# Cross attention of a gated block: the second exponential written over the scores in PSUM, in two halves, each split and waited for by itself

## The chip, the cores and the metric

The kernel runs on one core of a Trainium2 chip. A core has TensorE (PE in the profile; its weight loads are listed apart as PEld), VectorE (DVE), ScalarE (ACT), GpSimd (POOL) and SyncE (SP), which here only starts transfers. Matrix products land in PSUM, whose 8 banks each hold 128 x 512 numbers of 32 bits; all else lies in SBUF. The metric is the device time of one launch, in microseconds (us). The median of 3 runs before the change is 2361.93 us (2361.77 to 2367.37).

## The reference, cut to what matters

The whole is a gated cross attention, a gated feed forward part, slots with 16 experts, and a second attention, over x of 8 blocks of 512 rows by 512. The change touches the first of these:

```
xn  = layer_norm(x);  ctx = layer_norm(context)
q   = (xn @ Wq) as 16 heads of 64, * 64 ** -0.5
k,v = split(ctx @ Wkv)                      # one head of keys and values for all 16
sim = q @ k.T, -inf where mask == 0
out = softmax(sim) @ v                      # per head
x1  = x + tanh(g_xattn) * (out @ Wout)      # then the feed forward part is added
```

## The kernel before, in words

**Numbers in two parts.** TensorE reads its operands in a shortened format (fp32r). To keep the precision, each operand is kept as a high part (the rounded value) and a low part (the value minus the high part), and each product is made of two or three products of parts. For the probabilities this means: ScalarE makes the exponential once into `prob_hi` (rounded as it is written) and once more, unrounded, into `prob`; VectorE subtracts one from the other into `prob_lo`.

**Blocks and pairs.** `cross_attention` goes over 8 blocks `b`, and in each over 8 pairs of heads `i` (64 pairs in all). Of each block the mask lets at most 128 keys through (another branch, not taken here, serves other masks), so the scores of one pair are two tiles of 128 keys x 512 queries: the tile `SC` (`att_scores`), two PSUM banks, one for each head of the pair (`odd` 0 and 1). A pair takes these steps, by line of the kernel before:

- PE `pair_scores` (L642, L645): eight products into both banks of SC.
- ACT `exponentials`: L786 `prob_hi`, then L787 `prob`, each over both banks at once (128 x 1024).
- DVE `low_probs_of`: L1006 `prob_lo = prob - prob_hi`, 128 x 1024.
- PE `pair_out`: L655, L656 (twice each, from `prob_hi`), then L659 twice (from `prob_lo`) into `OB` (`att_out`). The value operand holds columns of ones, so OB holds the sums of the exponentials too.
- ACT `logarithms`, `inverses`: L794 twice, L798, which make one over the sums as exp(-ln(sum)) in `inv`.
- DVE `normalise` (L1013, twice) into `acc`; POOL L911 and L913 split `acc` into `oT_hi` and `oT_lo`, operands of the output products (L675).

**Order of the work.** Each engine has its own queue, written out by hand, and runs it strictly in order; semaphores join them. Between `pair_scores` and `pair_out` of a pair PE does the 12 query products of the next block (L591) and its maxima (L621); in the last block it does output products there (L675). ACT's order in a pair is L794, L794, L798 (of the pair before), L786, L787, then L772 (high part of the next block's queries). DVE's is L1013 twice (of the pair before), L1006, L998 (maxima), L992 (low part of the queries). After pair 7 of a block PE does the last maxima (L621) of the next block, which wait until L998 has read those before them, then turns x (L554) and makes outputs (L675).

**Semaphores that the change touches.** `probs` counts finished L787s, `low_probs` finished L1006s. PE waits for `low_probs` ahead of the first L659, and for `probs` ahead of the next `pair_scores` and of the first output products, since these overwrite SC. `prob` also serves, at the start of the program, as the place for one quarter of the raw Wq.

Of the kernel before, what the change touches and what calls it, by code (L numbers as in the profile page):

```python
# [7 lines left out]
ALU = mybir.AluOpType  # L8
ACT = mybir.ActivationFunctionType
AX = mybir.AxisListType  # L10

P = 128
B, S, D = 8, 512, 512
# [3 lines left out]
HP = H // 2  # L17
# [9 lines left out]
def plain(ap):  # L27

    return ap.bitcast(F32)


def products(hi_lo_w, hi_lo_m):

    (w_hi, w_lo), (m_hi, m_lo) = hi_lo_w, hi_lo_m
    return ((w_hi, m_hi), (w_hi, m_lo), (w_lo, m_hi))
# [280 lines left out]
def cross_attention(nc, whole, taken, I, ident, gates, many, first, x1_d, xnT_d, t_d, PIECES):  # L316
# [4 lines left out]
    with ExitStack() as stage:  # L321
        mem = Memory(nc, stage, whole, taken)
# [41 lines left out]
        m_heads = mem.sbuf("m_heads", [P, S], F32R)  # L364
        m_rows = mem.sbuf("m_rows", [P, TT, MC])
        mem.sbuf("m_rows_to_next_line", [P, LINE // 2 // 4])
        prob = mem.sbuf("prob", [P, 2, S])
        prob_hi = mem.sbuf("prob_hi", [P, 2, S], F32R)
        prob_lo = mem.sbuf("prob_lo", [P, 2, S], F32R)
        inv = mem.sbuf("inv", [P, 2, S])  # L370
        acc = mem.sbuf("acc", [P, 2, S])
        oT_hi = mem.sbuf("oT_hi", [P, HP, S], F32R)
        oT_lo = mem.sbuf("oT_lo", [P, HP, S], F32R)
        x_rows = mem.sbuf("x_rows", [P, TT, D])
        piece_place = [mem.sbuf(f"piece_{n}", [P, 4, P], F32R) for n in ("sum", "high")]

        SC, MX, OB = (pair_bank(n) for n in ("att_scores", "att_maxima", "att_out"))
        G = [mem.bank(f"att_general{i}") for i in range(2)]

        two = lambda ap: ap.rearrange("p i s -> p (i s)")  # L380
        raw_wkv = inv[:, 0, :].rearrange("p (k n) -> p k n", k=KT)
        raw_wq = [two(x_rows[:, 0:2, :]), two(x_rows[:, 2:4, :]), two(prob[:, :, :]), two(acc[:, :, :])]
        raw_wo = raw_wq[0:2]
        wkv_parts = [(slice(0, DH), slice(0, DH)), (slice(DH, 3 * DH), slice(0, P))]
        gam_rows = inv[0:2 * KT, 1, 384:384 + P]
# [28 lines left out]
        scores, hi_probs, probs, low_probs, heads_out, inv_ready, heads_taken, o_done, out_ready, x_added = (  # L414
            mem.sem(n) for n in ("scores", "hi_probs", "probs", "low_probs", "heads_out", "inv_ready", "heads_taken", "o_done", "out_ready", "x_added"))
# [25 lines left out]
        def out_banks(b):  # L441
            return [G[0][:, :], G[1][:, :], MX[:, 0, :], MX[:, 1, :]] if b >= late else [SC[:, 0, :], SC[:, 1, :], MX[:, 0, :], MX[:, 1, :]]
# [5 lines left out]
        with nc.Block() as block:  # L448
# [86 lines left out]
            def _(pe):  # L535
# [96 lines left out]
                def pair_scores(b, i):  # L632
                    pe.wait_ge(g_free, turned("q", b, i))
                    if i == 0:
                        pe.wait_ge(m_heads_ready, b + 1)
                        if 1 <= b <= late:
                            pe.wait_ge(x_added, (b - 1) * TT + 2)
                    if b or i:
                        pe.wait_ge(probs, b * HP + i)
                    for n, (kk, q) in enumerate(products((k_hi[b % 2], k_lo[b % 2]), (q_hi, q_lo))):  # L640
                        for half, odd in zip(halves, range(2)):
                            nc.tensor.matmul(SC[:, odd, :], kk[half, :], q[half, i, :], start=n == 0, stop=False)  # L642
                    for half, odd in zip(halves, range(2)):
                        at = odd * DH + i
                        last = nc.tensor.matmul(SC[:, odd, :], minus[half, at:at + 1].to_broadcast([DH, P]), m_heads[half, :], start=False, stop=True)  # L645
                    last.then_inc(scores, 1)

                def pair_out(b, i):
                    hi, lo = v_hi[b % 2], v_lo[b % 2]
                    cols = [slice(DH, 3 * DH), slice(0, P)]  # L650
                    pe.wait_ge(hi_probs, b * HP + i + 1)
                    if b or i:
                        pe.wait_ge(heads_taken, b * HP + i)
                    for odd in range(2):
                        nc.tensor.matmul(OB[:, odd, :], hi[:, cols[odd]], prob_hi[:, odd, :], start=True, stop=False)  # L655
                        nc.tensor.matmul(OB[:, odd, :], lo[:, cols[odd]], prob_hi[:, odd, :], start=False, stop=False)  # L656
                    pe.wait_ge(low_probs, b * HP + i + 1)
                    for odd in range(2):
                        last = nc.tensor.matmul(OB[:, odd, :], hi[:, cols[odd]], prob_lo[:, odd, :], start=False, stop=True)  # L659
                    last.then_inc(heads_out, 1)  # L660

                def output(b, i, tiles=range(TT)):
                    pe.wait_ge(o_done, b * HP + i + 1)
                    banks = out_banks(b)
                    for t in tiles:
                        if i == 0 and b > late:
                            pe.wait_ge(x_added, late * TT + t + 1)
                        if i == 0 and t == 0 and b == late:
                            pe.wait_ge(g_free, len(order))
                        if i == 0 and t == 0 and b < late:  # L670
                            pe.wait_ge(probs, (b + 1) * HP)
                        if i == 0 and t == 2 and b <= late:
                            pe.wait_ge(max_taken, (b + 2) * HP)
                        for n, (o, w) in enumerate(products((oT_hi, oT_lo), (wo_hi, wo_lo))):
                            last = nc.tensor.matmul(banks[t], o[:, i, t * P:(t + 1) * P], w[:, i, :],  # L675
                                                    start=i == 0 and n == 0, stop=i == HP - 1 and n == 2)
                        if i == HP - 1:
                            last.then_inc(out_ready, 1)

                def last_outputs(b):  # L680
                    pe.wait_ge(o_done, (b + 1) * HP)
                    for t in range(TT):
                        output(b, HP - 2, [t])
                        output(b, HP - 1, [t])
# [74 lines left out]
            def _(act):  # L759
# [21 lines left out]
                def exponentials(b, i):  # L781
                    bias = first_bias[:, b:b + 1]
                    act.wait_ge(scores, b * HP + i + 1)
                    if b or i:
                        act.wait_ge(heads_out, b * HP + i)
                    nc.scalar.activation(two(prob_hi[:, :, :]), two(SC[:, :, :]), ACT.Exp, bias=bias).then_inc(hi_probs, 1)  # L786
                    nc.scalar.activation(two(prob[:, :, :]), two(SC[:, :, :]), ACT.Exp, bias=bias).then_inc(probs, 1)  # L787

                def logarithms(b, i):
                    act.wait_ge(heads_out, b * HP + i + 1)  # L790
# [134 lines left out]
            def _(dve):  # L925
# [76 lines left out]
                    nc.vector.tensor_copy(m_heads[0:MC, :], OB[0:MC, 0, :]).then_inc(m_heads_ready, 1)  # L1002

                def low_probs_of(b, i):
                    dve.wait_ge(probs, b * HP + i + 1)
                    nc.vector.tensor_tensor(two(prob_lo[:, :, :]), two(prob[:, :, :]), two(plain(prob_hi[:, :, :])), ALU.subtract).then_inc(low_probs, 1)  # L1006

                def normalise(b, i):
                    dve.wait_ge(inv_ready, b * HP + i + 1)
# [2076 lines left out]
def gated_block(nc, I, out):  # L3086
# [6 lines left out]
    with ExitStack() as whole:  # L3093
# [18 lines left out]

        taken = []
        x1_begun = cross_attention(nc, whole, taken, I, ident, gates, many, first, x1_d, xnT_d, t_d, made_pieces)
        with nc.sbuf_tensor("bo_place", [P, D], F32R) as bo_place:
            pass
# [45 lines left out]
```

## Time and profile before

| | us |
|---|---|
| median of 3 runs | 2361.93 |
| the profiled execution's own time | 2363.39 |
| its span, from first to last instruction | 2361.6 |
| PE busy / share of the span | 2097.8 / 89% |
| DVE busy | 1328.9 / 56% |
| ACT busy | 673.9 / 29% |
| POOL busy | 618.8 / 26% |
| L659, the products with `prob_lo`, first and last start | 61.3, 624.8 |

The profile follows one execution. A busy share says how long an engine held work, not whether others waited for it. Matmuls overlap in their pipeline: a 128 x 512 product is shown as some 0.39 us, while the next one starts 0.23 us later, so PE can look nearly full in a stretch in which it also waits. What PE loses is therefore best read from the distance between starts.

### The profile page before, as it was taken

The numbers are of one execution on the slowest core, as the hardware profiler recorded it, in microseconds if no ns is written. First come the engines' busy times: TensorE is split into PE (matmuls) and PEld (weight loads), VectorE is DVE, ScalarE is ACT, GpSimd is POOL, SyncE is SP. The second block draws the span as 40 slices with busy tenths as digits, with TensorE's granted clock in tenths as the row PEclk, the third lists the DMA queues.
The fourth block names the chain that finished last, engine by engine and source line by source line (L and its number), as shares of the span: only waits on it lengthen the run. The fifth ranks groups of instructions, "written<-read, shape, count | busy, mean of one in ns | idle before, by whom it ended". The sixth has DMA issues, their size and how long they took to land. (4 is left out here: it accounts for less than half of the span.)

```text
span 2361.6 us, 29531 instructions
## 1 busy us (share of the span) xinstructions
PE 2097.8 (89%) x11170; PEld 1586.7 (67%) x11170; DVE 1328.9 (56%) x2127; ACT 673.9 (29%) x1068; POOL 618.8 (26%) x553
## 2 busy tenths in 40 slices
PE   7999999999989999999999999998998445454898
PEld 6777777777778788888888888887873111111577
DVE  7766666656457777667767676666651000000387
ACT  3644465446443331112111211123421000000231
POOL 5544565435377831310132000000320000000010
PEclk9999999999999999999999999999998767687899
DMA  4133223332296668665866494434879999999767
GB/s 166 70 104 131 103 65 107 118 107 74 91 393 243 240 267 338 226 207 194 340 225 212 178 357 161 160 125 167 321 289 431 433 426 432 432 433 430 277 235 264
DMA packets 181338, 565.10 MB, mean 239 GB/s; under 512 B 14256, under 2 KB 97752, under 8 KB 151352
## 3 DMA queue, kind: packets, MB, share of 16 engines
q1 hardware_dynamic: 172936, 504.37, 56.4%
q10 hardware_dynamic: 8272, 58.99, 5.9%
q8 instruction: 82, 1.34, 0.2%
q14 instruction: 48, 0.39, 0.1%
HBM read 450.07 MB, written 113.25 MB: 239 GB/s over the span
## 5 line engine op out<-in xcount | busy, mean ns | idle before, releaser
L1475 PE MATMUL ff_down<-w,u 128*128 128x512 f32 x1536 | 362.0, 394 | 8.5 <-DVE ff_x L1748 8.5
L1415 PE MATMUL ff_up<-ff_t,w 128*128 128x512 f32 x1488 | 357.6, 389 | 2.0 <-ACT ff_gate L1548 2.0
L1475 PEld LDWEIGHTS ff_down<-w,u 128*128 128x128 f32 x1536 | 291.0, 190 | 73.4 <-DVE ff_x L1748 12.6
L1415 PEld LDWEIGHTS ff_up<-ff_t,w 128*128 128x128 f32 x1488 | 279.2, 188 | 60.3 <-issue 2.4
L1748 DVE SCALAR_TENSOR_TENSOR ff_x<-ff_down,gates,ff_x 128x512 f32<-128x512 f32 x256 | 191.0, 749 | 86.8 <-PE ff_down L1475 85.3
L1415 PE MATMUL ff_up<-ff_b,w 128*128 128x512 f32 x954 | 234.3, 389 | 0.0
L2532 PE MATMUL e_down<-e_w,e_ug 128*32 128x512 f32 x480 | 74.7, 779 | 179.5 <-DMA e_w<-in_L_ffn_e_W 94.6
L1415 PEld LDWEIGHTS ff_up<-ff_b,w 128*128 128x128 f32 x954 | 179.1, 188 | 37.2
L2532 PEld LDWEIGHTS e_down<-e_w,e_ug 128*32 128x32 f32 x480 | 18.5, 138 | 234.2 <-issue 134.8
L1540 ACT ACTIVATE ff_gate<-ff_gate 128x512 f32<-128x512 f32 x62 | 39.2, 633 | 410.8 <-DVE ff_gate L1724 410.8
L2197 POOL TENSOR_TENSOR yn_lo<-y,yn_hi 128x2048 fp32r<-128x2048 f32 x8 | 36.7, 4592 | 437.6 <-ACT yn_hi L2155 437.6
L2640 DVE TENSOR_TENSOR e_u_rows<-e_turned,e_b1T 128x128 f32<-128x128 f32 x16 | 4.7, 292 | 260.0 <-PE e_turned L2523 260.0
L2985 POOL TENSOR_TENSOR v_pairs<-v_biased,c_odd_rows 128x512 f32<-128x512 f32 x2 | 2.5, 1286 | 491.7 <-DVE v_biased L3062 491.7
L1013 DVE TENSOR_TENSOR acc<-att_out,inv 64x512 f32<-64x512 f32 x128 | 88.1, 688 | 67.3 <-ACT inv L798 65.6
L913 POOL TENSOR_TENSOR oT_lo<-acc,oT_hi 128x512 fp32r<-128x512 f32 x64 | 115.2, 1801 | 9.4 <-issue 0.5
L1559 ACT COPY ff_gate<-ff_up 128x512 f32<-128x512 f32 x62 | 36.5, 589 | 271.1 <-PE ff_up L1415 271.1
L94 POOL TENSOR_TENSOR ff_t_sum<-ff_t_sum,ff_t_high 128x512 f32<-128x512 f32 x20 | 28.4, 1421 | 310.8 <-DMA ff_t_high<-xnT 310.8
L1006 DVE TENSOR_TENSOR prob_lo<-prob,prob_hi 128x1024 fp32r<-128x1024 f32 x64 | 80.2, 1253 | 52.1 <-ACT prob L787 51.9
L591 PE MATMUL att_general<-nT_hi,wq_hi 128*128 128x512 f32 x252 | 106.5, 423 | 0.4 <-DVE nT_lo L962 0.4
L794 ACT ACTIVATE inv<-att_out 64x512 f32<-64x512 f32 x128 | 75.9, 593 | 90.6 <-PE att_out L659 89.9
L2593 ACT COPY e_y_parts<-e_down 128x512 f32<-128x512 f32 x16 | 9.4, 586 | 321.1 <-PE e_down L2532 311.5
L591 PE MATMUL att_general<-nT_hi,wq_lo 128*128 128x512 f32 x252 | 99.8, 396 | 0.0
(482 smaller groups left out, 4385.9 us busy)
## 6 DMA issues: line engine op xcount, KB each, us to landing
w<-ff_w_factors SPq DMA_DIRECT2D x48, 1792.0 KB, 7.4
e_wg<-in_L_ffn_e_Wg SPq DMA_DIRECT2D x15, 4096.0 KB, 25.7
e_w<-in_L_ffn_e_W SPq DMA_DIRECT2D x14, 4096.0 KB, 20.0
e_w<-in_L_ffn_e_W ACTq DMA_DIRECT2D x13, 4096.0 KB, 50.3
ff_w_factors<-w SPq DMA_DIRECT2D x15, 1792.0 KB, 6.9
w<-ff_w_parts SPq DMA_DIRECT2D x48, 512.0 KB, 4.8
ff_t<-ff_t_factors SPq DMA_DIRECT2D x16, 1024.0 KB, 13.9
e_w<-in_L_ffn_e_W SPq DMA_DIRECT2D x16, 1024.0 KB, 9.8
```

Source lines behind the costliest of these rows:

```text
L591: last = nc.tensor.matmul(bank[:, :], w[:, k, i * P:(i + 1) * P], m[:, k, :], start=k == 0 and n == 0, stop=k == KT - 1 and n == 2)
L794: nc.scalar.activation(inv[halves[odd], i % 2, :], OB[halves[1 - odd], odd, :], ACT.Ln)
L913: nc.gpsimd.tensor_tensor(oT_lo[:, i, :], acc[:, i % 2, :], plain(oT_hi[:, i, :]), ALU.subtract).then_inc(o_done, 1)
L1006: nc.vector.tensor_tensor(two(prob_lo[:, :, :]), two(prob[:, :, :]), two(plain(prob_hi[:, :, :])), ALU.subtract).then_inc(low_probs, 1)
L1013: last = nc.vector.tensor_tensor(acc[half, i % 2, :], OB[half, odd, :], inv[half, i % 2, :], ALU.mult)
L1415: last = nc.tensor.matmul(bank[:, :], a, m, start=start and c == 0, stop=stop and c == 5)
L1475: last = nc.tensor.matmul(DN[m % 2][:, :], a, w, start=c == 0, stop=c == 5)
L1540: nc.scalar.activation(g, DN[n][:, :] if n < PLAIN else g, ACT.Silu).then_inc(gate1_done, 1)
L1559: nc.scalar.copy(gate0[n % 2][:, :], up_bank(n, A11_B11)[:, :]).then_inc(p1_kept, 1)
L1748: v.scalar_tensor_tensor(place, DN[m % 2][:, :], gates[:, 0:1], place, ALU.mult, ALU.add).then_inc(down_taken, 1)
L2197: nc.gpsimd.tensor_tensor(yn[1][:, b % 2], y[:, :, :], plain(yn[0][:, b % 2]), ALU.subtract).then_inc(yn_lo_done, 1)
L2532: last = nc.tensor.matmul(YB[q * QW:(q + 1) * QW, :], ug[:, j * Q + q, :], w2[i][:, q * J + j, :], start=j == 0, stop=j == J - 1)
```

## The change

The second exponential no longer goes to `prob` in SBUF: it is written over the scores it reads, in PSUM, as two instructions of 128 x 512, one for each head. A drain of ACT stands ahead of them, since they overwrite what the first exponential reads. DVE's subtraction is cut in two in the same way and reads SC. Each half has its own count of `probs` and of `low_probs`, so both counts run to 2 x 64, and PE waits for each half ahead of the L659 that uses it. What overwrites SC now waits for `low_probs`. The tile `prob` stays as `wq_place` with its other use alone, so that nothing else moves in memory.

```diff
-        prob = mem.sbuf("prob", [P, 2, S])
+        wq_place = mem.sbuf("wq_place", [P, 2, S])
@@ pair_scores
                     if b or i:
-                        pe.wait_ge(probs, b * HP + i)
+                        pe.wait_ge(low_probs, 2 * (b * HP + i))
@@ pair_out
-                    pe.wait_ge(low_probs, b * HP + i + 1)
                     for odd in range(2):
+                        pe.wait_ge(low_probs, 2 * (b * HP + i) + odd + 1)
                         last = nc.tensor.matmul(OB[:, odd, :], hi[:, cols[odd]], prob_lo[:, odd, :], start=False, stop=True)
@@ output
                         if i == 0 and t == 0 and b < late:
-                            pe.wait_ge(probs, (b + 1) * HP)
+                            pe.wait_ge(low_probs, 2 * (b + 1) * HP)
@@ exponentials
                     nc.scalar.activation(two(prob_hi[:, :, :]), two(SC[:, :, :]), ACT.Exp, bias=bias).then_inc(hi_probs, 1)
-                    nc.scalar.activation(two(prob[:, :, :]), two(SC[:, :, :]), ACT.Exp, bias=bias).then_inc(probs, 1)
+                    act.drain()
+                    for odd in range(2):
+                        nc.scalar.activation(SC[:, odd, :], SC[:, odd, :], ACT.Exp, bias=bias).then_inc(probs, 1)
@@ low_probs_of
-                    dve.wait_ge(probs, b * HP + i + 1)
-                    nc.vector.tensor_tensor(two(prob_lo[:, :, :]), two(prob[:, :, :]), two(plain(prob_hi[:, :, :])), ALU.subtract).then_inc(low_probs, 1)
+                    for odd in range(2):
+                        dve.wait_ge(probs, 2 * (b * HP + i) + odd + 1)
+                        nc.vector.tensor_tensor(prob_lo[:, odd, :], SC[:, odd, :], plain(prob_hi[:, odd, :]), ALU.subtract).then_inc(low_probs, 1)
```

ACT's queue over one pair of block 0, before (L794 and L798 are the logarithms and the inverse, L772 is the high part of the queries):

```order
L786 ACTIVATE prob_hi<-att_scores,first_bias 128x1024 [waits heads_out,scores]
L787 ACTIVATE prob<-att_scores,first_bias 128x1024
L772 ACTIVATE q_hi<-att_general 128x512 [waits g_ready]
L794 ACTIVATE inv<-att_out 64x512 [waits heads_taken,heads_out]
L794 ACTIVATE inv<-att_out 64x512
L798 ACTIVATE inv<-inv 128x512
```

and after the change, the same place (lines further down are numbered 2 higher):

```order
L786 ACTIVATE prob_hi<-att_scores,first_bias 128x1024 [waits heads_out,scores]
L789 ACTIVATE att_scores<-att_scores,first_bias 128x512 x2
L772 ACTIVATE q_hi<-att_general 128x512 [waits g_ready]
L796 ACTIVATE inv<-att_out 64x512 [waits heads_taken,heads_out]
L796 ACTIVATE inv<-att_out 64x512
L800 ACTIVATE inv<-inv 128x512
```

One instruction over two banks has become two over one bank each, with SC as their output; nothing has moved past anything else. The drain is not a row of the order.

PE's queue at the end of a pair and the start of the next, as the difference of the two:

```order
 L655 MATMUL att_out<-prob_hi,v_hi 128x512
 L656 MATMUL att_out<-prob_hi,v_lo 128x512
-L659 MATMUL att_out<-prob_lo,v_hi 128x512 [waits low_probs]
-L659 MATMUL att_out<-prob_lo,v_hi 128x512
-L642 MATMUL att_scores<-q_hi,k_hi 128x512 [waits probs,g_free]
+L659 MATMUL att_out<-prob_lo,v_hi 128x512 [waits low_probs] x2
+L642 MATMUL att_scores<-q_hi,k_hi 128x512 [waits low_probs,g_free]
```

The products are the same in the same order; the second L659 has a wait of its own, and the next pair's scores wait for another semaphore.

## Rows read from the trace of the kernel before

**Rows 1.** Busy time by engine, 55 to 640 us: PE, PEld, DVE, ACT, POOL, clock, DMA share, GB/s.

```profile
55.00:640.00 585.00, 574.95 (x2883) 437.32 (x2881) 369.41 (x556) 303.53 (x423) 282.08 (x242) 1.00 0.28 95
```

**Rows 2.** Who waited for whom, 55 to 630 us: total us, times, longest.

```profile
PEld att_out L659 <- DVE prob_lo L1006: 17.3, 54, 1.0
...
PE att_maxima L621 <- DVE m_rows L998: 4.3, 7, 0.6
```

**Rows 3.** Timeline of ACT and DVE, one pair of block 2: start, us, instruction, idle before.

```profile
246.45 1.20 ACT L794 ACTIVATE inv<-att_out 64x512 f32<-64x512 f32 x2 [1.30 <-PE att_out L659]
247.72 0.63 ACT L798 ACTIVATE inv<-inv 128x512 f32<-128x512 f32 x1
248.26 1.10 ACT L786 ACTIVATE prob_hi<-att_scores,first_bias 128x1024 fp32r<-128x1024 f32 x1
249.26 1.10 ACT L787 ACTIVATE prob<-att_scores,first_bias 128x1024 f32<-128x1024 f32 x1
...
252.44 0.60 ACT L794 ACTIVATE inv<-att_out 64x512 f32<-64x512 f32 x1 [1.32 <-PE att_out L659]
...
250.39 1.23 DVE L1006 TENSOR_TENSOR prob_lo<-prob,prob_hi 128x1024 fp32r<-128x1024 f32 x1 [0.62 <-ACT prob L787]
```

**Rows 4.** Timeline of PE, end of five pairs: 2.0, 1.1, 6.6, 4.3, 7.3.

```profile
221.36 0.39 PE L656 MATMUL att_out<-prob_hi,v_lo 128*128 128x512 f32 x1
...
222.13 0.50 PE L642 MATMUL att_scores<-q_hi,k_hi 64*128 64x512 f32 x2
...
150.99 0.40 PE L656 MATMUL att_out<-prob_hi,v_lo 128*128 128x512 f32 x1
...
151.81 0.50 PE L642 MATMUL att_scores<-q_hi,k_hi 64*128 64x512 f32 x2
...
562.75 0.40 PE L656 MATMUL att_out<-prob_hi,v_lo 128*128 128x512 f32 x1
...
563.59 0.50 PE L642 MATMUL att_scores<-q_hi,k_hi 64*128 64x512 f32 x2
...
391.87 0.40 PE L656 MATMUL att_out<-prob_hi,v_lo 128*128 128x512 f32 x1
...
393.15 0.50 PE L642 MATMUL att_scores<-q_hi,k_hi 64*128 64x512 f32 x2
...
597.69 0.39 PE L656 MATMUL att_out<-prob_hi,v_lo 128*128 128x512 f32 x1
...
599.01 0.51 PE L642 MATMUL att_scores<-q_hi,k_hi 64*128 64x512 f32 x2
```

**Rows 5.** One line each: how often, ns min/median/max, first and last start.

```profile
L764 ACT ACTIVATE nT_hi<-att_general,gam x28: 677/689/692, 50.9 to 502.2; 128x512 fp32r<-128x512 f32 x28
...
L772 ACT ACTIVATE q_hi<-att_general x63: 580/598/603, 23.1 to 567.8; 128x512 fp32r<-128x512 f32 x63
...
L967 DVE TENSOR_TENSOR cT_lo<-att_general,cT_hi x7: 684/692/692, 60.8 to 506.0; 128x512 fp32r<-128x512 f32 x7
...
L1006 DVE TENSOR_TENSOR prob_lo<-prob,prob_hi x64: 1224/1226/1672, 59.6 to 621.0; 128x1024 fp32r<-128x1024 f32 x64
...
L913 POOL TENSOR_TENSOR oT_lo<-acc,oT_hi x64: 1270/2083/2172, 70.9 to 629.9; 128x512 fp32r<-128x512 f32 x64
```

**Rows 6.** Timeline of all engines after pair 7 of blocks 2 and 6.

```profile
263.62 1.23 DVE L998 TENSOR_REDUCE m_rows<-att_maxima 128x8 f32<-128x1024 f32 x1
...
264.99 0.71 PE L621 MATMUL att_maxima<-k_max,q_hi 128*128 128x256 f32 x4 [0.62 <-DVE m_rows L998]
...
567.64 1.60 DVE L1006 TENSOR_TENSOR prob_lo<-prob,prob_hi 128x1024 fp32r<-128x1024 f32 x1 [0.62 <-ACT prob L787]
```

**Rows 7.** Busy time by engine, 88 to 96 us, columns as in the first group.

```profile
88.00:92.00 4.00, 1.61 (x6) 0.97 (x6) 3.08 (x4) 2.72 (x4) 2.14 (x2) 1.00 0.00 0
92.00:96.00 4.00, 4.00 (x15) 2.61 (x14) 2.72 (x4) 3.42 (x5) 4.00 (x3) 0.57 0.00 0
```

**Rows 8.** Timeline of SP's queue behind the last block: first load of the next stage.

```profile
643.20 0.94 SPq L1269 DMA_DIRECT2D ff_raw<-in_L_xattn_Wff  x2
```

More of the change, by code:

```diff
@@ L381, in cross_attention @@
         raw_wkv = inv[:, 0, :].rearrange("p (k n) -> p k n", k=KT)
-        raw_wq = [two(x_rows[:, 0:2, :]), two(x_rows[:, 2:4, :]), two(prob[:, :, :]), two(acc[:, :, :])]
+        raw_wq = [two(x_rows[:, 0:2, :]), two(x_rows[:, 2:4, :]), two(wq_place[:, :, :]), two(acc[:, :, :])]
         raw_wo = raw_wq[0:2]
```

## The prediction

> **What bounds the kernel now.** I read the busy shares by engine first. In the stretch from 55 to 640 us, where all 64 pairs lie, PE is busy 574.95 of 585 us at full clock, and ACT, DVE and POOL are each busy 48 to 63% [rows 1]. So PE sets the time, and the change adds nothing to PE's own work. What it can win is the time that PE waits here, about which the busy share says little, since overlapping matmuls cover short waits.
>
> The table of waits names what the change touches: 54 weight loads of L659 wait for the subtraction L1006, 17.3 us in all, and 7 times the maxima L621 wait for L998, 0.62 us each [rows 2]. A waiting weight load is not yet lost time, for it normally runs under the matmul ahead of it. So I take the loss from distances between starts: from the last L656 of a pair to the first L642 of the next. Where nothing is late (pair 0 of a block) it is 222.13 - 221.36 = 0.77 us. In an ordinary pair it is 0.82 to 0.84 (151.81 - 150.99, the first of them, and 563.59 - 562.75, the last); in a late one 393.15 - 391.87 = 1.28; in the last block 599.01 - 597.69 = 1.32 [rows 4].
>
> The reason is a ring through three engines. L794 of one pair starts at 246.45, of the next at 252.44: 5.99 us [rows 3]. Between them lie L794, L798, L786, L787, L1006 and the two L659. PE's own work for a pair is 5.93 (5.99 less the 0.06 it waits), so ring and PE run almost level. In the last block PE has less to do between, and the ring alone sets 5.99.
>
> **The change, part by part.** I count from the start h of L786, 248.26 in the pair shown. L786 ends at h + 1.10, L787 starts at h + 1.00, L1006 at h + 2.13, and it ends at 250.39 + 1.23 = 251.62, h + 3.36 [rows 3].
>
> *The drain.* L798 follows L794 behind a drain: 247.72 against an end at 246.45 + 1.20, 0.07 us later, while L787 without one starts 0.10 before L786 ends [rows 3]. The first in-place exponential starts at h + 1.17.
>
> *The two exponentials.* No row shows ACT writing PSUM. The nearest are L764 (128 x 512 from PSUM, an operand per partition, as the bias is here), 0.69 us, and L772 (a constant in its place), 0.60 [rows 5]. L798 reads SBUF and takes 0.63 [rows 3], so the SBUF side costs 0.03 more than PSUM where it is read; if writing is alike, 0.66. That is the value I take, with 0.60 below and 0.69 above; the far upper end is the 1.10 of L787 for each half [rows 3], where reading and writing one bank would hinder each other. The halves run h + 1.17 to 1.83 and 1.73 to 2.39. ACT's row is 0.29 us longer than before, which costs nothing: behind it ACT waits 1.32 for L659 [rows 3].
>
> The Trainium skill speaks against cutting: VectorE: DVE Perf Modes, in its section on the TRN2 errata, says that the fixed cost is paid per instruction, once for a large tile and again for every small one. ScalarE: Activation LUTs (What ACT_TABLE_LOAD costs) gives 280 ns + 0.833 ns per element with such a bias: 707 ns for 512, an estimate that is 0.02 over L764's row; the same page (Step-by-step: what each stage is for) calls PSUM the faster destination. By 0.71 the sum below would be 6.8 instead of 7.5.
>
> *The two subtractions.* L967 is the same operation (one operand in PSUM, one in SBUF, fp32r out, 128 x 512): 0.69 us [rows 5]. From L787's end to L1006's start there are 0.03. The first half runs h + 1.86 to 2.55, the second, a short 0.03 behind it, h + 2.58 to 3.27. That is 0.09 earlier than the 3.36 of before, between 0.15 (exponential of 0.60) and 0.06 (0.69). DVE's busy time grows by 0.15 a pair, and it still stands idle 0.62 ahead of L1006 [rows 3].
>
> *The split wait.* Only the second L659 needs the second half; the first runs before it. In the ring one matmul of 0.23 drops out. Together the ring shortens by 0.32, to 5.67.
>
> *Stretched subtractions.* L1006 has a median of 1.23 and a maximum of 1.67 [rows 5]; it is 1.60 in pair 7 of block 6 [rows 6]. L967 and L764's kind, with a PSUM operand, show nothing such (684 to 692 over 7, at times when POOL works). So I count the stretch as gone. POOL's L913 takes 1.27 to 2.17 [rows 5], the long ones beside L1006. The Trainium skill (SBUF — State Buffer, SBUF: two separate sides) gives the rule: a VectorE instruction with two SBUF inputs and a GpSimd one lock each other out for the whole instruction. By that rule L913 should fall to 1.3 throughout; the sum does not use it, for nothing on PE waits for POOL.
>
> *The waits of pair_scores and output* on low_probs instead of probs: already met, since the L659 ahead of them in PE's queue has waited for the same count. Nothing.
>
> What PE gets back, by groups of pairs:
> - 31 ordinary pairs of blocks 1 to 6 lose 0.05 to 0.08, 2.0 us together; a ring of 5.67 is below PE's 5.93, all returns: 2.0.
> - Five late pairs there (1.3, 2.3, 3.3, 4.3, 5.3): one loses 0.51 [rows 4], four 0.31 to 0.34. The 0.32 and the stretch gone cover all: 1.8.
> - Block 0 loses 1.6 in pairs 1 to 6 by the same distances, 0.95 of it in pair 4. An estimate: the 0.32 there, pairs 2 and 3 (0.3 together) whole, 0.1 of the rest: 0.7.
> - Last block: six pairs lose 0.54 to 0.57, more than 0.32: 6 x 0.32 = 1.9.
> - Block ends, seven: L998 starts when the subtraction ends and L621 waits for it, so this moves with the subtraction: 7 x 0.09 = 0.6, and the 0.37 stretch of the one at 567.64 [rows 6]: 1.0.
>
> Sum 7.4, with roundings 7.5 us. Behind the last pair the next stage's first load is issued at 643.20 [rows 8], after the last x1 stores in SP's queue, so later stages start earlier by the same amount. The profiled execution would go from 2363.39 to 2355.9 (span 2361.6 to 2354.1); on the median of 2361.93 that gives **2354.4 us**. With the exponential at 0.60 or 0.69, thirteen places (six in the last block, seven block ends) move by 0.06 or 0.03: 8.2 to 7.1 us.
>
> **Rivals.**
>
> *A, only the split wait pays.* Drain, second ACT start-up and second DVE start-up eat the 0.09. Last block 6 x 0.23 = 1.4, block ends 0.4 (the one stretch), block 0 0.5, blocks 1 to 6 still 3.8: 6.1 us, 2355.8. For it: the 0.09 is a small remainder of parts worked out from neighbouring lines. Against: it needs exponentials of 0.75, longer than L764.
>
> *B, in place is slow (the other side).* If reading and writing the same bank doubles an exponential to 1.10, the second subtraction ends at h + 4.00, 0.64 late; less 0.23, the ring is 6.40. Some 42 pairs of blocks 0 to 6 lose 0.4 (17 us, less 1.3 for the stretches), the last block 2.4, seven block ends 0.64 each (4.5), the starts of blocks 0.8: +23 us, 2385. It decides from about 0.90 us per exponential: 1.17 + 0.90 + 0.80 + 0.03 + 0.69 = 3.59, 0.23 late, and the ring is 5.99 again. For it: no row shows ACT writing PSUM. Against: PE adds into a bank, a read and a write of each element, at 0.23 us for 512 columns, three times ACT's pace.
>
> *C, given back later.* The feed forward stage has waits of its own on loads, and the whole gain might go there: 2361.9. Against: those loads hang on the end of this stage [rows 8].
>
> *D, a clock gain beside it.* From 92 to 96 us the granted clock is 0.57, behind a stretch (pair 4 of block 0) in which PE is busy only 1.61 of 4 us [rows 7]. Should the shorter wait avoid that, 4 x 0.43 = 1.7 us more: 2352.7. Against: most of that wait stays.
>
> **How the numbers follow.** My forecast 0.50, A 0.22, B 0.10, C 0.08, D 0.10. A measurement can tell about 0.3%, 7.1 us, from no change; the forecast lies just beyond. I put three quarters of it beyond that (0.38), with D and a little of A: faster 0.50. The rest of it, A and C: same 0.40. B: slower 0.10. The range holds forecast, A, D and C: 2350.5 to 2362.0; left out are B and what lies beyond D. The forecast's own range is 2353 to 2356.
>
> **What would show it.** Right: the two in-place rows at 0.60 to 0.69 us each, the first 0.07 after L786's end; subtractions of 0.69 with the second ending at h + 3.2 to 3.3; L656 to next L642 at 0.77 in blocks 1 to 6 and about 1.0 in the last; the ring there 5.67; the waits of L659's weight loads mostly gone. Wrong: exponentials over 0.75 (A) or 0.90 (B); a subtraction still stretched beside POOL; L642 starting late on low_probs; the stage shorter by 7 us but the span not (C).

## The result, and the profile after

Over six runs of each on the same chip, the median went from 2361.85 us (2360.41 to 2367.37) to 2347.64 us (2343.34 to 2352.53): ratio 0.9936, 95% interval 0.9924 to 0.9948. That is 14.2 us faster, nearly twice the 7.5 us forecast and below the range given. The profiled execution took 2349.44 us (span 2347.6). A second set, shown below as e4, gave 2349.42 us and a ratio of 0.9952 (0.9938 to 0.9967), so 11.8 us.

The table of waits, 55 to 630 us, has columns as in [rows 2]: total us, times, longest.

```profile
PEld att_out L659 <- DVE prob_lo L1009: 2.5, 9, 0.4
...
PE att_maxima L621 <- DVE m_rows L1000: 2.5, 7, 0.4
```

The waits of L659's weight loads fell from 17.3 us in 54 cases to 2.5 in 9, and each of the seven waits of L621 from 0.62 to about 0.35. The busy time over the same window as [rows 1]:

```profile
55.00:640.00 585.00, 577.83 (x2923) 447.91 (x2920) 370.41 (x623) 317.55 (x492) 247.36 (x247) 1.00 0.29 100
```

PE's busy time says little (577.83 against 574.95, and the window now holds some work of the next stage). POOL's is the one that moved much: 282.1 to 247.4. The reason is in the lines: times, ns min/median/max, first and last start.

```profile
L789 ACT ACTIVATE att_scores<-att_scores,first_bias x128: 652/658/662, 58.6 to 608.8; 128x512 f32<-128x512 f32 x128
...
L1009 DVE TENSOR_TENSOR prob_lo<-att_scores,prob_hi x128: 678/686/695, 59.3 to 609.5; 128x512 fp32r<-128x512 f32 x128
...
L915 POOL TENSOR_TENSOR oT_lo<-acc,oT_hi x64: 1265/1291/1303, 69.8 to 618.1; 128x512 fp32r<-128x512 f32 x64
```

The in-place exponentials take 0.66 us each, the subtractions 0.69, and none of the 128 is stretched. POOL's subtraction, 1270/2083/2172 in [rows 5], is now 1.29 throughout.

One pair of block 2, ACT, then DVE, as in [rows 3] (start, us, instruction, idle before). L786 starts at h = 243.55:

```profile
243.55 1.10 ACT L786 ACTIVATE prob_hi<-att_scores,first_bias 128x1024 fp32r<-128x1024 f32 x1
244.73 1.24 ACT L789 ACTIVATE att_scores<-att_scores,first_bias 128x512 f32<-128x512 f32 x2
245.89 0.60 ACT L772 ACTIVATE q_hi<-att_general 128x512 fp32r<-128x512 f32 x1
247.69 1.20 ACT L796 ACTIVATE inv<-att_out 64x512 f32<-64x512 f32 x2 [1.20 <-PE att_out L659]
```

```profile
245.43 1.29 DVE L1009 TENSOR_TENSOR prob_lo<-att_scores,prob_hi 128x512 fp32r<-128x512 f32 x2 [0.36 <-ACT att_scores L789]
246.63 1.22 DVE L1000 TENSOR_REDUCE m_rows<-att_maxima 128x8 f32<-128x1024 f32 x1
```

Two things stand in the last two rows that the forecast did not have. The two subtractions take 1.29 together, less than 2 x 0.686 = 1.37: the second starts before the first has ended, and they end at h + 3.17. And the maxima L1000 start at 246.63, while the subtractions end at 245.43 + 1.29 = 246.72.

PE at the end of that pair, and of a pair of the last block, as in [rows 4]:

```profile
246.80 0.40 PE L656 MATMUL att_out<-prob_hi,v_lo 128*128 128x512 f32 x1
247.03 0.62 PE L659 MATMUL att_out<-prob_lo,v_hi 128*128 128x512 f32 x2
247.58 0.50 PE L642 MATMUL att_scores<-q_hi,k_hi 64*128 64x512 f32 x2
...
587.61 0.39 PE L656 MATMUL att_out<-prob_hi,v_lo 128*128 128x512 f32 x1
587.84 0.72 PE L659 MATMUL att_out<-prob_lo,v_hi 128*128 128x512 f32 x2
588.49 0.50 PE L642 MATMUL att_scores<-q_hi,k_hi 64*128 64x512 f32 x2
```

From L656 to L642 it is 0.78 in all pairs of blocks 1 to 6 (0.82 to 1.28 before) and 0.88 in the last block (1.32).

**Where the 14 us are.** I measured the stage from the first L642 to the last L659. It was 568.6 us in the first profile of the kernel before, 567.4 in a second one (e8), and is 556.9 now (557.0 in e4). The rest of the span behind it was 1736.8 and 1738.3, and is now 1734.6 and 1738.2: no change that stands out of its own scatter. So 10.4 to 11.7 us of the gain is in this stage. The table holds all of it; block 0 is read from e8 and e4, which both lack a half-clock stretch there, the other rows from the first two profiles:

| us | before | after | gained | forecast |
|---|---|---|---|---|
| block 0, with its end | 82.7 | 81.1 | 1.6 | 0.8 |
| pairs of blocks 1 to 6 | | | 3.7 | 3.8 |
| ends of blocks 1 to 5, each | 29.50 | 29.17 | 0.33 | 0.09 |
| end of block 6 | 6.84 | 6.15 | 0.69 | 0.46 |
| last block | 49.2 | 46.7 | 2.5 | 1.9 |
| sum | | | 10.2 | 7.4 |
| stretch at the lower clock in block 0, in the first profile before but not in e8 | | | 1.5 | 0 |

An end of a block is counted from pair 7's last L656 to the next block's first L642; for the pairs of blocks 1 to 6 it is what the blocks gained less their ends. The forecast's own roundings make 7.5 of the 7.4.

### The profile page after: what moved, and what is told of

Its sections match the earlier page's. It is cut to its first block and busy times, and to the rows that moved or that the text cites. A ratio compares the mean times of both kernels' runs of the same rounds, so it can differ in the third digit from the quotient of the medians.

```text
span 2347.6 us, 29723 instructions
## 1 busy us (share of the span) xinstructions
PE 2095.2 (89%) x11170; PEld 1590.9 (68%) x11170; DVE 1328.9 (57%) x2191; ACT 684.3 (29%) x1132; POOL 578.7 (25%) x553
## 5 line engine op out<-in xcount | busy, mean ns | idle before, releaser
L94 POOL TENSOR_TENSOR ff_t_sum<-ff_t_sum,ff_t_high 128x512 f32<-128x512 f32 x20 | 28.0, 1400 | 309.4 <-DMA ff_t_high<-xnT 309.4
L1009 DVE TENSOR_TENSOR prob_lo<-att_scores,prob_hi 128x512 fp32r<-128x512 f32 x128 | 82.5, 686 | 35.4 <-ACT att_scores L789 35.1
L591 PE MATMUL att_general<-nT_lo,wq_hi 128*128 128x512 f32 x252 | 99.7, 395 | 0.0
```

The costliest lines, as they stand in the source:

```text
L94: nc.gpsimd.tensor_tensor(total, total, rest, ALU.add)
L591: last = nc.tensor.matmul(bank[:, :], w[:, k, i * P:(i + 1) * P], m[:, k, :], start=k == 0 and n == 0, stop=k == KT - 1 and n == 2)
L1009: nc.vector.tensor_tensor(prob_lo[:, odd, :], SC[:, odd, :], plain(prob_hi[:, odd, :]), ALU.subtract).then_inc(low_probs, 1)
```

## The experiments

The theory after the first result (Q in the expectations): two VectorE instructions in a row overlap by 0.084 us unless the start partition of their PSUM (or SBUF) operand changes. Before the change L1006 read only SBUF, so the last PSUM operand ahead of L998 was that of the second `normalise`, at partition 64. L998, at partition 0, had to wait for L1006's end. Now L1009 reads PSUM at partition 0, and L1000 starts early. The rivals: (P) the overlap depends on PSUM against SBUF inputs or on the instruction's length; and for the gain as a whole, that it comes from the place (PSUM), from the halves, or from PE's split wait alone.

**e1: halves, but in SBUF.** The in-place writing is undone, the halves stay.

```diff
-                    act.drain()
-                        nc.scalar.activation(SC[:, odd, :], SC[:, odd, :], ACT.Exp, bias=bias).then_inc(probs, 1)
+                        nc.scalar.activation(wq_place[:, odd, :], SC[:, odd, :], ACT.Exp, bias=bias).then_inc(probs, 1)
-                        nc.vector.tensor_tensor(prob_lo[:, odd, :], SC[:, odd, :], plain(prob_hi[:, odd, :]), ALU.subtract).then_inc(low_probs, 1)
+                        nc.vector.tensor_tensor(prob_lo[:, odd, :], wq_place[:, odd, :], plain(prob_hi[:, odd, :]), ALU.subtract).then_inc(low_probs, 1)
```

> The changed kernel, but the second exponential goes to SBUF as before, in two halves without a drain; subtractions halved, waits by half. Theory Q (a VectorE instruction may start 0.08 us before the end of the one ahead if its inputs start at the same partitions as the last ones read from that memory): the two subtractions start 0.61 us apart, as in the changed kernel, but L998 starts 0.03 after the second one, since the last PSUM input ahead of it (L1013's second) started at partition 64. Rival P (the overlap comes from reading PSUM): the subtractions start 0.70 apart. Both: exponentials of 0.69, the first at h + 1.00; second subtraction ends at h + 3.02 (Q) or 3.13 (P) against 3.17; the last block's ring 5.45 or 5.52 against 5.56. Subtractions are stretched again beside POOL, L913 back at 2.1 us. Time within 1 us of the changed kernel by both: about 2347.

Measured: 2386.67 us (4 runs), ratio 1.0111 (1.0095 to 1.0127). I had expected it as fast as the change; it is 25 us slower than the kernel before, and the stage took 594.9 us. Timeline of DVE and POOL in a pair of block 2, first with the two subtractions merged, then each by itself, and two of its lines:

```profile
237.71 0.61 POOL L913 CAST oT_hi<-acc 128x512 fp32r<-128x512 f32 x1 [2.04 <-DVE acc L1016]
...
237.84 2.73 DVE L1009 TENSOR_TENSOR prob_lo<-wq_place,prob_hi 128x512 fp32r<-128x512 f32 x2 [0.19 <-ACT wq_place L788]
...
238.48 1.54 POOL L915 TENSOR_TENSOR oT_lo<-acc,oT_hi 128x512 fp32r<-128x512 f32 x1
...
240.60 1.23 DVE L1000 TENSOR_REDUCE m_rows<-att_maxima 128x8 f32<-128x1024 f32 x1
```

```profile
237.84 1.03 DVE L1009 TENSOR_TENSOR prob_lo<-wq_place,prob_hi 128x512 fp32r<-128x512 f32 x1 [0.19 <-ACT wq_place L788]
...
238.79 1.78 DVE L1009 TENSOR_TENSOR prob_lo<-wq_place,prob_hi 128x512 fp32r<-128x512 f32 x1
```

```profile
L1009 DVE TENSOR_TENSOR prob_lo<-wq_place,prob_hi x128: 677/1029/1783, 56.8 to 645.2; 128x512 fp32r<-128x512 f32 x128
...
L915 POOL TENSOR_TENSOR oT_lo<-acc,oT_hi x64: 1267/1539/1557, 68.0 to 653.9; 128x512 fp32r<-128x512 f32 x64
```

Both halves are held up. The first takes 1.03 instead of 0.68: POOL's L913 had started 0.13 ahead of it. POOL's L915 starts at 238.48, while the first half still runs (to 238.87), and lasts to 240.02, 0.25 more than the 1.29 that it takes in the changed kernel. The second half starts at 238.79, takes 1.78 and is done only at 240.57, 2.73 after the first began. With one whole subtraction in the kernel before it was POOL that waited (L913 at 2.08, [rows 5]); with two, POOL gets in between them and DVE waits, on PE's path. The Trainium skill (SBUF — State Buffer, SBUF: two separate sides) says that a VectorE instruction with two SBUF inputs and a GpSimd one lock each other out for a whole instruction. The trace agrees: the second half ends 0.55 behind L915, less than the 0.68 that it takes undisturbed and far less than the 1.78 it took here. On the overlap: L1000 starts 240.60 - 240.57 = 0.03 behind the subtraction's end, as theory Q has it. Where POOL stays out, the second half starts 0.608 behind the first, as it does in PSUM, which speaks against rival P. The stage of this run also holds a longer stretch at the lower clock than the others (the granted clock is 0.71, 0.50 and 0.93 over 88 to 100 us), which I estimate at twice the 1.5 us of e8's paragraph.

**e2: in place, but whole.** One exponential and one subtraction of 128 x 1024 in PSUM; the counts go up by two.

```diff
-                    for odd in range(2):
-                        nc.scalar.activation(SC[:, odd, :], SC[:, odd, :], ACT.Exp, bias=bias).then_inc(probs, 1)
+                    nc.scalar.activation(two(SC[:, :, :]), two(SC[:, :, :]), ACT.Exp, bias=bias).then_inc(probs, 2)
-                        nc.vector.tensor_tensor(prob_lo[:, odd, :], SC[:, odd, :], plain(prob_hi[:, odd, :]), ALU.subtract).then_inc(low_probs, 1)
+                    nc.vector.tensor_tensor(two(prob_lo[:, :, :]), two(SC[:, :, :]), two(plain(prob_hi[:, :, :])), ALU.subtract).then_inc(low_probs, 2)
```

> The changed kernel, but the in-place exponential and the subtraction are one instruction each of 128 x 1024. Theory Q: exponential 1.07 us from h + 1.18 to 2.25, subtraction 1.23 to h + 3.51 (3.36 before, 3.17 changed), L998 starts 0.08 before its end. The ring is 6.14 us, over PE's 5.93; the attention stage is 3 to 6 us longer than before and 15 to 18 longer than changed: about 2366. Rival (PSUM as the place is what pays): at least half of the gain stays, 2355 or less. L913 1.29 in all pairs by both.

Measured: 2375.56 us (5 runs), ratio 1.0053 (1.0038 to 1.0068). The stage took 579.6 us, 11 more than before, where 3 to 6 had been expected. The subtraction started 0.10 us behind the exponential's end instead of 0.03; it ends at h + 3.60, and the last block's ring is 6.23 where I had 6.14. In e9 below, where the counts go up by one, it is 0.03 again and the stage 574.8: the 0.07 in each of 64 pairs (4.5 us) comes with the step of two and makes up most of the 4.8 between them.

**e3: the change, but both L659 wait for both halves.**

```diff
-                        pe.wait_ge(low_probs, 2 * (b * HP + i) + odd + 1)
+                        pe.wait_ge(low_probs, 2 * (b * HP + i) + 2)
```

> The changed kernel, but both L659 wait for both halves. Subtraction end stays h + 3.17, PE reaches L659 at h + 3.25 in blocks 1 to 6: no loss there. In the last block one matmul of 0.23 comes back into the ring, 5.79 against 5.56: +1.4 us in all, about 2349. Rival (the split wait is what pays): 5 us or more lost.

Measured: 2352.18 us (7 runs), ratio 0.9963 (0.9950 to 0.9975). The stage took 558.7 us, 1.8 more than with the change; 1.4 had been expected. PE in the last block:

```profile
588.36 0.39 PE L656 MATMUL att_out<-prob_hi,v_lo 128*128 128x512 f32 x1
588.83 0.73 PE L659 MATMUL att_out<-prob_lo,v_hi 128*128 128x512 f32 x2
589.49 0.50 PE L642 MATMUL att_scores<-q_hi,k_hi 64*128 64x512 f32 x2
```

The first L659 now stands 0.47 behind L656 where it was 0.23, and L656 to L642 is 1.13. The last block's ring is 5.80 against 5.56: the whole 0.23 of the split wait shows there, 1.4 us in six pairs; the other 0.4 is in block 0. In blocks 1 to 6 nothing changed (0.78). So the split wait is worth 1.8 of some 11 us.

**e4: the change again**, for the part behind the stage.

> The changed kernel itself, once more. Stage until the last L659: 613.0 us again within 0.1, no half-clock stretch at 92 us. What follows the stage took 1734.6 us in its first profile against 1736.8 before; if these 2.2 us are a gain of the change they stand again, if they are chance of the later stages they move by 2 us or more between profiles.

Measured: 2349.42 us (5 runs), ratio 0.9952 (0.9938 to 0.9967). The stage is 556.95 us again (556.87 before), the rest 1738.2 instead of 1734.6. By the measure set above, what the first profile of the change had gained behind the stage (2.2 us) was chance.

**e5 and e6: a shorter first wait of PE in block 0**, without and with the change. ACT's five deviations of the context are issued at pair 4 instead of pair 3.

```diff
-                        if b == 0 and i == 3:
+                        if b == 0 and i == 4:
```

> The kernel before; ACT's deviations for block 2 (in block 0) are made one pair later, so that the logarithms of pair 3 do not wait on DVE's statistics. Theory K (the shorter PE wait around 88 us is what takes away the half-clock stretch, and with it 1.6 us): normalise of pair 3 still waits until DVE is free at 87.2, PE waits 1.0 instead of 1.95 us, no granted clock under 1.00 from 92 to 96; block 1 starts 3.2 us earlier (1.5 of it by the wait). Rival (the stretch is not tied to this wait): clock 0.57 again there, 1.5 us earlier.

Measured: 2360.0 us (10 runs), ratio 0.9988 (0.9977 to 0.9998). PE's wait fell to 1.06 us as expected, and the pair with it took 7.52 us against 9.00 in e8: 1.5. There is no stretch at the lower clock behind it. But block 0 as a whole took 81.76 us against 84.14 in the first profile and 82.67 in e8, 2.4 less than the first and not the 3.2 expected: its first pair took 9.06 instead of 8.43, with the granted clock at 0.58 over 52 to 56 us, a stretch that neither of the two profiles of the kernel before has.

> The changed kernel with the same move of the deviations. PE waits 0.6 instead of 1.8 us in pair 4 of block 0; the stage ends 1.5 us earlier, last L659 at 611.6; about 2348 by the median of e4.

Measured: 2346.24 us (6 runs; 2343.45 to 2352.52), ratio 0.9933 (0.9916 to 0.9950). This is the lowest median of all, but block 0 took 80.91 us against 81.00 and 81.14 with the change alone, and the stage (556.8) is no shorter. The wait did what was expected: it fell from 1.69 to 0.66 us, and its pair took 6.93 instead of 8.29, 1.4 less. The block's first pair took it back, 9.71 instead of 8.43, under a lower clock that the change's own two profiles do not show there:

```profile
56.00:60.00 4.00, 4.00 (x20) 2.98 (x17) 2.40 (x9) 2.87 (x4) 0.00 (x0) 0.82 0.88 283
```

So this profile can't say whether the move is worth 1.4 us on top of the change, and the median does not stand apart from the change's.

**e7: the kernel before, with the two normalising products in reverse order**, so that the last PSUM operand ahead of L1006 and L998 starts at partition 0. No time, size or place changes.

```diff
-                    for half, odd in zip(halves, range(2)):
+                    for half, odd in reversed(list(zip(halves, range(2)))):
```

> The kernel before; normalise takes its two halves in the other order, so that its last PSUM input starts at partition 0 instead of 64. Theory Q: L998, held 0.03 behind L1006 before, starts 0.08 before its end; each of seven block ends is 0.11 shorter, 0.8 us in all. Rival P (overlap needs a PSUM operand in the instruction ahead): L998 starts 0.03 behind L1006 as before, nothing changes.

Timeline of DVE in one pair of block 2, then at the end of block 1 with POOL:

```profile
249.71 1.23 DVE L1006 TENSOR_TENSOR prob_lo<-prob,prob_hi 128x1024 fp32r<-128x1024 f32 x1 [0.62 <-ACT prob L787]
...
250.86 1.22 DVE L998 TENSOR_REDUCE m_rows<-att_maxima 128x8 f32<-128x1024 f32 x1
```

L1006 ends at 250.94 and L998 starts at 250.86, 0.08 before it. In the kernel before it starts 0.03 behind, the subtraction reading SBUF and 1.23 long in both. So the order of two other instructions sets whether these two overlap: Q holds, P is refuted. The Trainium skill has this rule (VectorE: DVE Perf Modes, Two Vector instructions with no wait between them): an instruction is held until all before it are done if an input of it starts in another quadrant (32 partitions) than the first input that the last instruction reading that memory took from there; the page calls this a model. The trace agrees, -0.084 us against +0.031, also where a semaphore's wait stands between the two and is already met. At the undisturbed ends of blocks it gave 0.05 to 0.09 us each (29.41 to 29.45 against 29.50), a little less than the 0.11 expected.

The time did not move: 2362.41 us (10 runs), ratio 0.9998 (0.9987 to 1.0010). Two block ends took 30.51:

```profile
184.31 1.29 POOL L94 TENSOR_TENSOR piece_sum<-piece_sum,piece_high 128x512 f32<-128x512 f32 x1 [3.53 <-DMA piece_high<-xnT]
...
184.39 2.29 DVE L1006 TENSOR_TENSOR prob_lo<-prob,prob_hi 128x1024 fp32r<-128x1024 f32 x1 [0.62 <-ACT prob L787]
...
186.61 1.21 DVE L998 TENSOR_REDUCE m_rows<-att_maxima 128x8 f32<-128x1024 f32 x1
```

POOL's L94 waits for a transfer, and by chance it starts 0.08 us ahead of pair 7's subtraction. That one then takes 2.29 us, and the block ends 1.1 us later. This happened twice in e7, once in e5 and not in the two profiles of the kernel before. With the subtractions reading PSUM it did not happen in any profile: in the change L94 runs beside them at the ends of blocks as well, once from 0.2 us ahead, and the longest of 128 is 0.695.

**e8: the kernel before again**, profiled once more.

> The kernel before, once more for its profile. Last L659 starts at 624.8 within 0.2; what follows differs by up to 2.5 us from the 1736.8 of the first profile, since the changed kernel's two profiles differ by 3.5. The half-clock stretch at 92 us is there again if it belongs to the 1.95 us wait ahead of it.

2359.89 us. The last L659 starts at 619.84, not at the 624.8 expected: the stage itself is only 1.2 shorter, but it starts at 52.48 instead of 56.22. Over all profiles its start lies between 52.5 and 56.2, whatever the kernel. Busy time around PE's long wait in block 0, columns as in [rows 1]:

```profile
84.00:88.00 4.00, 1.45 (x6) 0.89 (x6) 2.84 (x4) 2.96 (x4) 1.90 (x2) 1.00 0.00 2
88.00:92.00 4.00, 4.00 (x21) 2.77 (x21) 2.96 (x4) 3.36 (x5) 4.00 (x3) 1.00 0.00 0
```

The same wait as in [rows 7] (PE is busy 1.45 of 4 us, there 1.61), and yet the granted clock stays at 1.00 behind it, where [rows 7] have 0.57. It is the same kernel. Block 0 took 82.67 us here and 84.14 there, so the stretch at the lower clock costs 1.5 us where it comes.

**e9: the place alone.** The kernel before with one whole exponential in place behind the drain and one whole subtraction from PSUM, counts going up by one.

```diff
-                    nc.scalar.activation(two(prob[:, :, :]), two(SC[:, :, :]), ACT.Exp, bias=bias).then_inc(probs, 1)
+                    act.drain()
+                    nc.scalar.activation(two(SC[:, :, :]), two(SC[:, :, :]), ACT.Exp, bias=bias).then_inc(probs, 1)
-                    nc.vector.tensor_tensor(two(prob_lo[:, :, :]), two(prob[:, :, :]), two(plain(prob_hi[:, :, :])), ALU.subtract).then_inc(low_probs, 1)
+                    nc.vector.tensor_tensor(two(prob_lo[:, :, :]), two(SC[:, :, :]), two(plain(prob_hi[:, :, :])), ALU.subtract).then_inc(low_probs, 1)
```

> The kernel before with only the place changed: drain, one exponential of 128 x 1024 over the scores, one subtraction from PSUM, semaphores counted by one (e2 counted them by two, and its subtraction started 0.10 us behind the exponential instead of 0.03). Theory: exponential 1.09 from h + 1.18, subtraction from h + 2.30 to 3.53, ring 6.16 (6.23 in e2), L998 0.08 before the subtraction's end, no stretched subtraction, L913 1.29. First L642 to last L659: 576 us (579.6 in e2, 568.6 before, 556.9 changed): 8 us slower than before. Rival (all of e2's loss beyond my first estimate is the count by two): 572.

Measured: 2368.49 us (10 runs), ratio 1.0027 (1.0013 to 1.0041). ACT and DVE of one pair, with h = 243.26:

```profile
243.26 1.10 ACT L786 ACTIVATE prob_hi<-att_scores,first_bias 128x1024 fp32r<-128x1024 f32 x1
...
244.44 1.09 ACT L788 ACTIVATE att_scores<-att_scores,first_bias 128x1024 f32<-128x1024 f32 x1
...
245.56 1.22 DVE L1007 TENSOR_TENSOR prob_lo<-att_scores,prob_hi 128x1024 fp32r<-128x1024 f32 x1 [0.79 <-ACT att_scores L788]
...
246.71 1.21 DVE L999 TENSOR_REDUCE m_rows<-att_maxima 128x8 f32<-128x1024 f32 x1
```

The drain puts the exponential at h + 1.18 instead of 1.00. The subtraction starts 0.03 behind it, as it does with a count by one in the kernel before, and ends at h + 3.53; the ring is 6.15 (6.16 expected), the stage 574.8 (576). The place alone, with the drain that it needs, costs some 6 us.

**e10: halves of the exponential alone**, in SBUF, with one whole subtraction behind both.

```diff
-                    for odd in range(2):
-                        dve.wait_ge(probs, 2 * (b * HP + i) + odd + 1)
-                        nc.vector.tensor_tensor(prob_lo[:, odd, :], wq_place[:, odd, :], plain(prob_hi[:, odd, :]), ALU.subtract).then_inc(low_probs, 1)
+                    dve.wait_ge(probs, 2 * (b * HP + i) + 2)
+                    nc.vector.tensor_tensor(two(prob_lo[:, :, :]), two(wq_place[:, :, :]), two(plain(prob_hi[:, :, :])), ALU.subtract).then_inc(low_probs, 1)
```

> As e1 (second exponential in two halves to SBUF, no drain), but one subtraction of 128 x 1024 that waits for both. Theory (e1 lost its time because POOL takes the port that both share between two short two-SBUF-input subtractions): subtraction h + 2.28 to 3.50, ring 6.13, stretched only where before was; first L642 to last L659 575 us, against 594.9 in e1. Rival (halving the exponentials itself costs e1's time): 590 or more.

Measured: 2371.1 us (10 runs), ratio 1.0038 (1.0025 to 1.0052). Ring 6.14, stage 578.1 (575 expected; several block ends in it took 1.1 more by the stretch seen in e7). That is 17 us below e1's 594.9, some 1.5 of it by e1's longer stretch at the lower clock; the two differ only in the cut of the subtraction and the waits by half that go with it. So most of e1's 26 us is the gap between two subtractions in SBUF. Halving the exponentials alone is not free either: the ring went from 5.99 to 6.14 and the stage from 568.6 to 578.1, some 3 of that by three stretched block ends.

Put together, the stage takes:

| second exponential | whole | in halves |
|---|---|---|
| in SBUF | 567.4, 568.6 | 594.9 (e1) |
| in PSUM, in place | 574.8 (e9) | 556.9 (e3, one wait: 558.7) |

e2, e9, e10 and the 568.6 hold the half-clock stretch of e8's paragraph (1.5 us), e1 one of twice the length, the others none. Each of the two edits alone loses, by 6 and by some 25 us against 568.6 when e1's longer stretch is allowed for; together they gain 10 to 12.

## Why the prediction came out too small

**Right, with numbers.** PE waiting for the subtraction was the bound, and the stage gained by shortening it. The first in-place exponential starts at h + 1.18 (1.17 forecast), the exponentials take 0.66 (0.66), the first subtraction starts at h + 1.88 (1.86) and takes 0.69 (0.69). No stretched subtraction is left. Ordinary and late pairs of blocks 1 to 6 gave 3.7 us (3.8). The split wait gave 0.24 in the last block's ring (0.23). POOL's subtraction fell to 1.29 (1.3).

**The step that failed** is in "The two subtractions": "the second, a short 0.03 behind it, h + 2.58 to 3.27". It starts 0.084 before the first one's end. I had taken the 0.03 from an instruction that waits for another engine; two on one engine overlap here. The subtractions of a pair end at h + 3.17, and the ring in the last block fell to 5.56 instead of 5.67: 6 x 0.11 = 0.65 us there, and a share of block 0's extra 0.8. That block's pairs were an estimate, and too low: pair 4 gained 0.71 us by the distance of pair starts (9.00 in e8, 8.29 now) where 0.32 was counted. 0.43 of it is the ring; the other 0.27 is a shorter wait ahead of L655 (1.96 to 1.69), for which the sum has no term.

**The term beside it** is "L998 starts when the subtraction ends", 0.09 for each block end. L1000 starts at h + 3.08 where L998 did at h + 3.40: 0.10 of it is the earlier end by the second subtraction's overlap, 0.115 the maxima's own, 0.09 was forecast. Together the seven ends gave 2.7 us against 1.0. e7 showed the maxima's overlap by itself.

**How much of the miss that is.** The forecast was 6.7 us short by the first medians and 4.3 by the second. Between the two first profiles, 14.0 us apart, the shortfall of 6.5 is made up so: 2.7 us in the stage, of which the two overlaps give 0.65 in the last block and 7 x 0.21 = 1.5 at the block ends; 1.5 us from the lower clock in block 0; and 2.2 us behind the stage, which is chance by e4. The overlaps are thus the step that was wrong in the reasoning, but only a third of the distance.

**The clock.** Rival D, with a chance of 0.10, forecast this size (1.7 us) but is not shown as the cause. The lower clock at 92 to 96 us [rows 7] is gone in the change:

```profile
88.00:92.00 4.00, 2.96 (x14) 1.73 (x14) 3.63 (x6) 3.09 (x6) 3.00 (x3) 1.00 0.00 0
92.00:96.00 4.00, 4.00 (x21) 3.37 (x20) 2.83 (x6) 3.62 (x6) 3.85 (x4) 1.00 0.00 0
```

But it was missing in e8 too, without any change. Of the seven profiles in which PE stands idle 1.8 to 2.2 us ahead of L655 and 0.6 us or more ahead of the L659 behind it (before, e1, e2, e7, e8, e9, e10) six had it; of the five in which the first of these is 1.7 us or less (after, e3 to e6) none had. That fits D's mechanism and is no proof of it. And the clock has other stretches of this kind: in e5, e6 and e7 one lies over the first pair of block 0 and makes it 0.6 to 1.3 us longer. So single stages compare to about 1.5 us only, unless the clock rows of both are read as well.

**What stays open.** The stage gave 10.4 to 11.7 us; the two medians say 14.2 and 11.8. The chance stretches at block ends, 1.1 us each and gone with the change, give up to some 2 in single executions. The part behind the stage took 1732.7 to 1739.2 us over all profiles, with no relation to the kernel. The part ahead of the stage took 52.5 to 56.2 us, again with no relation to it. Whether the remaining 0 to 4 us are one of these or something else, these runs can't say.

**The rivals.** A (only the split wait pays) is refuted: e3 keeps over 80% of the stage's gain without it. B (in place slow) is refuted for both lengths, at 0.66 and 1.09 us. C (given back later) is refuted: what follows the stage took 1734.6 and 1738.2 us with the change, 1736.8 and 1738.3 before. The split wait is the main part of the last block's ring, as forecast (0.24 of the 0.43), but the smaller part of the whole: 1.8 us of the stage's 10 to 12. The rest hangs on the halves being in PSUM.

The range was too narrow at the fast side. Its lower end came from the exponential's length and D, but had no bound for how one DVE instruction follows another, though [rows 3] only showed starts that waited for another engine.

## What to carry to other kernels

An instruction on the ring is worth cutting in two, so that the next engine's part overlaps it, but only where no third engine can get in between: with both operands in SBUF POOL took the gap and cutting the subtraction lost some 15 us (e10 to e1), with one in PSUM cutting exponential and subtraction won some 15 (e9 to e3). Before pricing a cut, find in the trace how two instructions in a row follow each other on that engine, not only how long each takes. And compare stages rather than spans: 10 us of 2350 were found to some 0.1 us from the starts of a few lines, while the part behind the stage moved by 6 us on its own and the part ahead by 4. Read the granted clock of each stretch beside it: e6's gain of 1.4 us in one pair was hidden by a lower clock in another.

## What the runs showed of the hardware

- VectorE starts the next instruction 0.084 us before the end of the one ahead, or 0.031 behind it, by the start partition of the operand last read from the same memory (e7 against the kernel before, 49 of 49 pairs); it was so with both inputs in SBUF or one in PSUM, and at 128 x 512 and 128 x 1024.
- Writing an exponential over its own input in PSUM costs nothing extra: 0.652 to 0.662 us for 128 x 512 against 0.67 to 0.69 with an SBUF output (e1), 1.09 for 128 x 1024 against 1.10 [rows 3].
- A VectorE subtraction with both inputs in SBUF and a GpSimd one hold each other up: 0.68 us became 1.03 and 1.78 beside L913 and L915 (e1), 1.23 became 2.29 behind a start of L94 by 0.08 us (e7). With one input in PSUM the longest of 128 is 0.695 and POOL's subtraction takes 1.29 instead of 2.08.
- A drain between two ACT instructions costs 0.18 us from start to start (h + 1.18 against 1.00): the second starts 0.08 behind the end of the first instead of 0.10 ahead of it.
- A semaphore that goes up by two in one step released its waiter 0.10 us behind the end of the instruction (e2), by one 0.03 (e9).
- After the same wait of about 2 us PE's granted clock went partly to the lower level in one execution (0.57 over 4 us) and stayed at 1.00 in another of the same kernel (e8).
